# A two-layer graph, LSTM and max-plus network on one core: constants loaded one stage ahead, registers read first, dense rounds of two tokens

## The reference

```
x = x + gnn0(ln(x), adj)     # elu of gate * normed adj @ (x theta) + (1 - gate) * x W_h
x = x + lstm(ln(x))          # H = 256, then an argmax-gated prefix and suffix sum, * fw_att, bw_att
x = x + gnn1(ln(x), adj)     # D^-1/2 (adj + I) D^-1/2 (x W) + b
x = x + ffn(ln(x))           # below, FFN = 1024, 8 pieces
t[f]  = max_d(x[d] + Wt[f, d]) + bt[f]
trop  = s * max_p(t sl_cvx + of_cvx) + (1 - s) * min_p(t sl_ccv + of_ccv)
out   = (g * trop + (1 - g) * gelu(x Wc + bc)) @ Wd + bd,   g = sigmoid(x Wg + bg)
```

## Time and profile before

| | |
|---|---|
| median of 3 runs | 6029.61 us (6028.96 to 6030.96) |
| the profiled execution | 6013.3 us, its span 6011.5 us |
| busy: PE, DVE, ACT, POOL | 91%, 83%, 56%, 28% of the span |
| granted TensorE clock, mean | 0.965 |
| DMA moved | 529 MB, 88 GB/s over the span |
| stages, from the trace | first graph 0 to 525.6; recurrent to 1552.8; second graph to 2161.5; tropical to 4455.8 (slots from 3661.6 and 4163.4, dense from 4421.3); last to 6011.5 |

### The profile page before, as it was taken

The page is one execution under the profiler, slowest core; times in us unless marked ns, Lnnn a source line. Parts: engine busy times, 40 slices in busy tenths (PEclk is TensorE's granted clock), DMA queues, the critical chain, the costliest instruction groups (busy, mean ns, idle before and its releaser), DMA issues. The chain is left out here.

```text
span 6011.5 us, 111926 instructions
## 1 busy us (share of the span) xinstructions
PE 5471.9 (91%) x33194; PEld 3624.3 (60%) x33194; DVE 4967.6 (83%) x9615; ACT 3371.2 (56%) x6793; POOL 1711.0 (28%) x3552
## 2 busy tenths in 40 slices
PE   9998999999899969999999985875759999999999
PEld 6666888888788856666666653443434444444444
DVE  8996664444699969999999997986859999999998
ACT  6664444444455546666666651221228787877787
POOL 3331000000255536666666651375530000000000
PEclk9999999999899989999999997987979999999999
DMA  4442001000355522222222211365541212222221
GB/s 136 135 135 69 0 11 50 0 0 0 96 176 176 177 90 73 73 73 73 73 73 72 71 67 32 114 219 179 171 161 66 89 63 85 69 84 83 71 84 49
DMA packets 359806, 529.10 MB, mean 88 GB/s; under 512 B 28256, under 2 KB 298208, under 8 KB 359680
## 3 DMA queue, kind: packets, MB, share of 16 engines
q1 hardware_dynamic: 323376, 401.62, 20.5%
q0 software_dynamic: 36304, 126.13, 6.1%
HBM read 298.52 MB, written 229.14 MB: 88 GB/s over the span
## 5 line engine op out<-in xcount | busy, mean ns | idle before, releaser
L1894 PE MATMUL t_fetched<-t_wpart,t_onehot 128*128 128x512 f32 x4096 | 1222.0, 420 | 35.8 <-DVE t_tout L1999 15.9
L1999 DVE SCALAR_TENSOR_TENSOR t_tout<-t_fetched,t_top,t_tout 128x1024 f32<-128x1024 f32 x896 | 1149.0, 1282 | 36.3 <-PE t_fetched L1894 4.8
L1894 PEld LDWEIGHTS t_fetched<-t_wpart,t_onehot 128*128 128x128 f32 x4096 | 691.8, 188 | 269.2 <-DVE t_tout L1999 131.2
L2832 DVE SCALAR_TENSOR_TENSOR f_line<-f_hinge,f_vec,f_line 128x1024 f32<-128x1024 f32 x512 | 655.2, 1280 | 82.5 <-ACT f_hinge L2710 48.3
L2322 PE MATMUL ts_fetched<-t_wpart,ts_onehot 128*128 128x512 f32 x1608 | 508.7, 451 | 165.2 <-ACT ts_onehot L2297 65.3
L961 PE MATMUL l_ps<-l_wih,l_x 128*64 128x128 f32 (+1 forms) x6144 | 531.6, 308 | 1.0 <-DVE l_ps L597 1.0
L2322 PEld LDWEIGHTS ts_fetched<-t_wpart,ts_onehot 128*128 128x128 f32 x1608 | 305.6, 208 | 316.6 <-DVE ts_tout L2390 202.3
L961 PE MATMUL l_ps<-l_whh,l_ht 128*64 128x128 f32 (+1 forms) x6144 | 492.6, 309 | 0.0
L2762 PE MATMUL f_pso<-f_fused,f_wd 128*128 128x512 f32 x1024 | 461.9, 594 | 23.1 <-DVE f_ox L2828 23.1
L2749 PE MATMUL f_psc<-f_x,f_wc 128*128 128x512 f32 x1024 | 482.8, 594 | 0.0
L925 ACT ACTIVATE l_act<-l_ps 128x128 f32<-128x128 f32 x1024 | 253.9, 276 | 407.0 <-PE l_ps L961 407.0
(11 more groups left out here) (384 smaller groups left out, 10720.8 us busy)
## 6 DMA issues: line engine op xcount, KB each, us to landing
t<-t_tout SPq DMA_DIRECT2D x128, 512.0 KB, 2.6
f_t<-t SPq DMA_DIRECT2D x64, 1024.0 KB, 5.3
g_adj<-in_adj SPq DMA_DIRECT2D x128, 256.0 KB, 3.0
g_adjt<-in_adjt SPq DMA_DIRECT2D x128, 256.0 KB, 2.7
t_x<-x_normalised SPq DMA_DIRECT2D x130, 128.0 KB, 2.3
g_x<-in_x SPq DMA_DIRECT2D x64, 256.0 KB, 2.8
x_kept<-g_x SPq DMA_DIRECT2D x64, 256.0 KB, 2.1
g_x<-x_kept SPq DMA_DIRECT2D x64, 256.0 KB, 2.8
```

What stands on the lines that cost most here:

```text
L1894: mm = pe.matmul(fetched[c % RING][:, h * CH:(h + 1) * CH], one_hot[g][:, c % GRP * P:(c % GRP + 1) * P], w_part[part][:, k, h * CH:(h + 1 ...
L1999: dve.scalar_tensor_tensor(t_out[j][:, :], column[:, :], value, t_out[j][:, :], ALU.add, ALU.max)\
L2832: dve.scalar_tensor_tensor(acc[:, :], source, column(u, "bend", k), acc[:, :], ALU.mult, ALU.add)\
```

## The change

Four edits. The buffers of a stage's weights are allocated outside it, and their loads are issued by SP during the stage before: the recurrent weights and biases at the end of the first graph stage (its identity is kept for all three), the second graph stage's logit weights and `fw`, `bw` at the end of SP's program in the recurrent stage, and the last stage's six loads at the start of the dense block. In the second graph stage the first input now goes ahead of the five constants that are still loaded there, and PE and DVE wait for these inside their rounds, ahead of the first reader. The slot stages read the class ends (PE: candidate offsets too) before the first selection, and each engine only what it uses: ACT, DVE and POOL 11 instead of 16. In the last stage ACT and DVE read the counts ahead of the wait for the loads. A dense round takes 2 tokens instead of 8.

```diff
@@ -214,6 +213,14 @@
             for n in range(1, X_RING):
                 load(x_in, a["x"], x_loaded, n, n)
+            for w, name in ((w_ih, "w_ih_t"), (w_hh, "w_hh_t")):
+                sp.dma_start(w[:, :, :, :, :].rearrange("p k q c u -> p k (q c u)"),
+                             a[name].rearrange("(k p) g -> p k g", p=P)).then_inc(lstm_in, 16)
+            for e, name in enumerate(("b_ih", "b_hh")):
+                for c2 in range(2):
+                    half_rows = slice(c2 * (P // 2), (c2 + 1) * (P // 2))
+                    sp.dma_start(bias[half_rows, e, :, :].rearrange("p q u -> p (q u)"),
+                                 a[name][c2:c2 + 1, :].to_broadcast([P // 2, GATES * P])).then_inc(lstm_in, 16)
             for j in range(2):
...
@@ -533,15 +535,6 @@
         def _(sp):
-            for w, name in ((w_ih, "w_ih_t"), (w_hh, "w_hh_t")):
-                sp.dma_start(w[:, :, :, :, :].rearrange("p k q c u -> p k (q c u)"),
-                             a[name].rearrange("(k p) g -> p k g", p=P)).then_inc(const_in, 16)
-            sp.dma_start(ident[:, :], a["ident"]).then_inc(const_in, 16)
-            for e, name in enumerate(("b_ih", "b_hh")):
-                for c2 in range(2):
-                    sp.dma_start(bias[c2 * HB:(c2 + 1) * HB, e, :, :].rearrange("p q u -> p (q u)"),
-                                 a[name][c2:c2 + 1, :].to_broadcast([HB, GATES * P])).then_inc(bias_in, 16)
...
+            sp.dma_start(graph_consts["w_lin"][:, :, :], a["w_lin_t"].rearrange("(k p) c -> p k c", p=P))\
+              .then_inc(graph_consts["loaded"], 16)
+            for t in range(NT):
+                sp.dma_start(graph_consts["b_lin"][:, t, :], a["b_lin"].to_broadcast([P, 2])).then_inc(graph_consts["loaded"], 16)
+            for name, src in (("fw", a["fw_att"].to_broadcast([P, D])), ("bw", a["bw_att"].to_broadcast([P, D]))):
+                sp.dma_start(graph_consts[name][:, :], src).then_inc(graph_consts["loaded"], 16)
...
@@ -587,7 +586,7 @@
-            dve.wait_ge(bias_in, 16 * 4)
+            dve.wait_ge(lstm_in, 16 * 6)
             dve.tensor_tensor(bias_sum[:, :, :], bias[:, 0, :, :], bias[:, 1, :, :], ALU.add).then_inc(bias_ready, 1)
...
@@ -1007,7 +1006,7 @@
-            pe.wait_ge(const_in, 16 * 3)
+            pe.wait_ge(lstm_in, 16 * 6)
...
@@ -1111,7 +1106,7 @@
-        CONST_DMAS = 11
+        CONST_DMAS = 5
...
@@ -1135,17 +1130,6 @@
         def _(sp):
-            sp.dma_start(w_lin[:, :, :], a["w_lin_t"].rearrange("(k p) c -> p k c", p=P)).then_inc(const_in, 16)
-            sp.dma_start(ident[:, :], a["ident"]).then_inc(const_in, 16)
-            for t in range(NT):
-                sp.dma_start(b_lin[:, t, :], a["b_lin"].to_broadcast([P, 2])).then_inc(const_in, 16)
-                sp.dma_start(b_all[:, t, :], a["b1"].to_broadcast([P, D])).then_inc(const_in, 16)
-            sp.dma_start(fw[:, :], a["fw_att"].to_broadcast([P, D])).then_inc(const_in, 16)
-            sp.dma_start(bw[:, :], a["bw_att"].to_broadcast([P, D])).then_inc(const_in, 16)
-            sp.dma_start(before[:, :], a["before"]).then_inc(const_in, 16)
-            sp.dma_start(after[:, :], a["after"]).then_inc(const_in, 16)
-            sp.dma_start(w[:, :, :], a["W1"].rearrange("(k p) e -> p k e", p=P)).then_inc(const_in, 16)
             def load(dst, src, loaded, n, j):
...
-            for j in range(2):
-                load(x1_in, x1_dram, x1_loaded, j, j)
-                load(adj_in, a["adj"], adj_loaded, j, j)
-                load(adjt_in, a["adjt"], adjt_loaded, j, j)
+            load(x1_in, x1_dram, x1_loaded, 0, 0)
+            sp.dma_start(before[:, :], a["before"]).then_inc(late_in, 16)
+            sp.dma_start(after[:, :], a["after"]).then_inc(late_in, 16)
+            load(x1_in, x1_dram, x1_loaded, 1, 1)
+            for t in range(NT):
+                sp.dma_start(b_all[:, t, :], a["b1"].to_broadcast([P, D])).then_inc(late_in, 16)
+            load(adj_in, a["adj"], adj_loaded, 0, 0)
+            load(adjt_in, a["adjt"], adjt_loaded, 0, 0)
+            sp.dma_start(w[:, :, :], a["W1"].rearrange("(k p) e -> p k e", p=P)).then_inc(late_in, 16)
+            load(adj_in, a["adj"], adj_loaded, 1, 1)
+            load(adjt_in, a["adjt"], adjt_loaded, 1, 1)
             rounds(sp, body)
...
@@ -1295,6 +1286,7 @@
+                    pe.wait_ge(late_in, 16 * 5)
                     pe.wait_ge(wh_ready, n + 1)
...
@@ -1393,6 +1385,7 @@
+                    dve.wait_ge(late_in, 16 * 5)
                     dve.tensor_tensor(x2b[j][:, :, :], x2[:, :, :], b_all[:, :, :], ALU.add).then_inc(x2b_ready, 1)
...
@@ -1460,7 +1453,7 @@
-DENSE_RUN = 8
+DENSE_RUN = 2
...
@@ -2227,13 +2220,24 @@
-        def classes(eng, slot_pair):
-            ends = [eng.value_load(bounds[0:1, k:k + 1], min_val=2, max_val=MOST) for k in range(K)]
-            cands = [0] + [eng.value_load(bounds[0:1, K + k:K + k + 1], min_val=1, max_val=CLASSES[0] * MOST)
-                           for k in range(K - 1)]
-            hots = [0] + [eng.value_load(bounds[0:1, 2 * K - 1 + k:2 * K + k], min_val=1, max_val=CLASSES[0] * MOST)
+        def class_ends(eng):
+            return [eng.value_load(bounds[0:1, k:k + 1], min_val=2, max_val=MOST) for k in range(K)]
+        def class_cands(eng):
+            return [0] + [eng.value_load(bounds[0:1, K + k:K + k + 1], min_val=1, max_val=CLASSES[0] * MOST)
                           for k in range(K - 1)]
+        def class_hots(eng):
+            return [0] + [eng.value_load(bounds[0:1, 2 * K - 1 + k:2 * K + k], min_val=1, max_val=CLASSES[0] * MOST)
+                          for k in range(K - 1)]
+        unused = [0] * K
+        def classes(eng, ends, cands, hots, slot_pair):
...
+            ends = class_ends(pool)
             held(3, selected, 1)
             y_gather(0, rows[:, 2, 0:1])
-            end = classes(pool, slot_pair)
+            end = classes(pool, ends, class_cands(pool), unused, slot_pair)
...
-            classes(act, slot_pair)
+            classes(act, class_ends(act), unused, class_hots(act), slot_pair)
...
+            ends, cands = class_ends(pe), class_cands(pe)
             spread(0, 0, 0, 0, GRP)
-            classes(pe, slot_pair)
+            classes(pe, ends, cands, class_hots(pe), slot_pair)
...
+            ends = class_ends(dve)
             select(0, 0, 16, 2)
-            classes(dve, slot_pair)
...
+        @block.sync
+        def _(sp):
+            for w, at in ((early["w_raw"][0], AT_WC), (early["w_raw"][1], AT_WG), (early["w_d"], AT_WD)):
+                sp.dma_start(w[:, :, :], rows_dram[:, at:at + D].rearrange("(u p) d -> p u d", p=P)).then_inc(early["loaded"], 16)
+            sp.dma_start(early["ident"][:, :], a["ident"]).then_inc(early["loaded"], 16)
+            sp.dma_start(early["vec"][:, :, :], rows_dram[:, AT_VEC:ROW].rearrange("(u p) q -> p u q", p=P))\
+              .then_inc(early["loaded"], 16)
+            sp.dma_start(early["b_d"][:, :], a["bd"]).then_inc(early["loaded"], 16)
         @block.gpsimd
...
@@ -2620,14 +2629,6 @@
         def _(sp):
-            for v, at in ((0, AT_WC), (1, AT_WG)):
-                sp.dma_start(turned_in(v)[:, 0:FT, :],
-                             rows_dram[:, at:at + D].rearrange("(u p) d -> p u d", p=P)).then_inc(const_in, 16)
-            sp.dma_start(w_d[:, :, :], rows_dram[:, AT_WD:AT_WD + D].rearrange("(u p) d -> p u d", p=P)).then_inc(const_in, 16)
-            sp.dma_start(ident[:, :], a["ident"]).then_inc(const_in, 16)
-            sp.dma_start(vec[:, :, :], rows_dram[:, AT_VEC:ROW].rearrange("(u p) q -> p u q", p=P)).then_inc(const_in, 16)
-            sp.dma_start(b_d[:, :], a["bd"]).then_inc(const_in, 16)
...
@@ -2671,12 +2672,12 @@
         def _(act):
+            more, _ = counts(act)
             act.wait_ge(const_in, 16 * CONSTS)
             act.activation(half_bg[:, :], vec[:, :, 1], ACT.Copy, scale=0.5).then_inc(half_ready, 1)
             act.wait_ge(half_ready, 1)
             evict(act, 0)
-            more, _ = counts(act)
...
@@ -2796,9 +2797,9 @@
         def _(dve):
+            more, before = counts(dve)
             dve.wait_ge(const_in, 16 * CONSTS)
             evict(dve, 1)
-            more, before = counts(dve)
```

More of the change, by code:

```diff
@@ L79, in end, with stage_gnn0 @@
         assert self.k == self.per, (self.k, self.per)
-def stage_gnn0(nc, a, hx, x1_dram):
+def stage_gnn0(nc, a, hx, x1_dram, ident, w_ih, w_hh, bias, lstm_in):
     sems = []
@@ L449, with stage_lstm @@
 FAR = 1.0e30
-def stage_lstm(nc, a, hx, rows_dram, key_dram, hinge_count, row_kept):
+def stage_lstm(nc, a, hx, ident, w_ih, w_hh, bias, lstm_in, graph_consts, rows_dram, key_dram, hinge_count, row_kept):
     T, U = N, 4
@@ L457, in stage_lstm @@
     LANE = 384
-    sems = []
+    sems = [lstm_in]
     with ExitStack() as ctx:
@@ L465, in sem @@
             return sems[-1]
-        w_ih = sb("l_wih", [P, KD, GATES, 2, P])
-        w_hh = sb("l_whh", [P, KD, GATES, 2, P])
-        bias = sb("l_bias", [P, 2, GATES, P])
```

(38 more changed lines are left out.)

34 lines of the change are left out of this document (12 added, 22 removed).

## The result

| | before | after |
|---|---|---|
| median, five runs each | 6030.2 us (6028.96 to 6031.02) | **5996.95 us** (5994.34 to 6003.9) |
| profiled execution, span | 6013.3 us, 6011.5 us | 5996.85 us, 5995.0 us |
| mean granted TensorE clock | 0.965 | 0.965 |

The ratio is **0.9948, 95% interval 0.9933 to 0.9962**: faster, by about 33 us of the 50.9 forecast. On the scale of the first median, 6029.61, the ratio gives 5998.3, just above the range's end of 5998.

A forecast was written before the change was run, and what follows sets the result against it. Seams between stages, where TensorE idles for loads and register reads, were taken as the bound. Gains 5.6 + 8.9 + 12.1 + 13.0 + 11.3 = 50.9 us gave a profile of 5962.4, median 5979 us, range 5968 to 5998.

The forecast's parts named there:

- 1, first seam: First graph to recurrent stage: weights and biases issued behind the last store let PE start earlier; gain 5.6 us.
- 2, second seam: Recurrent to second graph stage: PE starts 9.9 us earlier, then stops 1.0 us for the late weight; gain 8.9 us.
- the waits in gnn1's loop: Second graph stage, two new waits in each of 64 rounds: taken as 0, at worst 4.5 us.
- 3, slots: Both slot stages: class bounds read ahead of the first selection bring first fetches forward 6.3 and 5.8 us; together 12.1.
- 4, dense uses: Dense block: two tokens a round leave 4 uses instead of 16, saving 12 steps, 14.6 us.
- 4, fill less gathers late: Dense block: shorter fill gains 0.4 us; gathers beside the last stage's loads come 2.0 us late.
- 5, last stage: Last stage's start: loads already landed and counts read first bring ACT's first line forward; gain 11.3 us, ends 9 and 13.
- a loop changing its pace: Sign against the forecast: it is wrong as a whole if a later stage's loop changes its pace.
- unfavourable end: Second seam's low case: the late weight lands when it did before, leaving a gain of 7.2 us.
- The slower rival: Second graph stage: fulfilled waits flush the engine, over 1.0 us a round makes the change slower; 6049 us at 1.1; 3%.
- The covers are short: Rival, 12%: DMAs moved into a stage delay it, losing 5.6, 3.0 and 1.7 us; gain 40.6 us, 5989 us.
- carried-over 16.3 us: Whole kernel: the median stood 16.3 us above the profiled execution, unexplained, and was assumed to do so again.

The follow-up runs named there:

- e6: Changed kernel plus idle instructions, 6 on DVE in the tropical constants and 30 on ACT in the dense block; 5968.91 us, ratio 0.992.
- e4: Kernel before plus only the slot stages' earlier register reads and the dense round of two tokens; 5993.98 us, ratio 0.9963.
- e10: Changed kernel plus `w` loaded behind the first x1, idle instructions (6 DVE, 30 ACT), last stage's loads issued in the tropical plan's block; 5961.03 us, ratio 0.9909.
- e3: Kernel before plus only the earlier loads for the recurrent and second graph stages; 6009.54 us, ratio 0.999.
- e12: Kernel before plus idle instructions, 4 on DVE ahead of `tropical_first` and 64 on ACT in the dense block; 6019.65 us (a single run).
- e5: Kernel before plus idle instructions, 10 on DVE in the tropical constants and 98 on ACT in the dense block; 6026.85 us, ratio 1.0016.

## Why the prediction was right and wrong

The terms, each as the mean over the profiles without and with the edit (14 in all):

| step | forecast | measured | from |
|---|---|---|---|
| 1, first seam | 5.6 | 5.0 | last copy to first gate 23.5 to 18.6 |
| 2, second seam | 8.9 | 6.7 | last hidden state to first `g_xn3t` 50.0 to 43.3 |
| the waits in gnn1's loop | 0 | -1.1 | loop 554.9 to 556.05 |
| third seam | 0 | -0.4 | last `g_xn3t` to first merge 47.2 to 47.6 |
| 3, slots | 12.1 | 11.9 | 96.1 to 89.8, and 34.2 to 28.6 |
| 4, dense uses | 14.6 | 14.3 | first to last use 20.3 to 6.0 |
| 4, fill less gathers late | 0.4 - 2.0 | -2.4 | last slot to first use 26.2 to 28.6 |
| 5, last stage | 11.3 | 10.6 | last use to ACT's first line 32.0 to 21.3 |
| loops not touched | 0 | -5.7 and -6.0 | `tropical_first` 1381.0 to 1386.6; ffn 1405.45 to 1411.5 |
| **sum** | **50.9** | **32.9** | the medians: 33.3 and 32.4 |

**The step that failed** is the sentence under the first bold words: the change leaves the bodies of the long loops as they are, so the forecast is a sum over five places. The bodies stayed, their places in the streams did not, and that cost 11.7 of the 18.0 us missing. The prediction named a loop changing its pace as what would make it wrong as a whole, but gave the untouched loops no term and no rival. The other 6.3 us are in the terms themselves: 2.2 in step 2, 1.1 in the loop's waits, 0.8 in the gathers and the fill, the rest in pieces under 1 us. Put right by idle instructions alone, the change gives 48.6 us (e6), but 3 of these come from an ffn loop that is even shorter than that of before. The five places by themselves measured 46.1 us, a tenth less than the 50.9 forecast.

**Step 1** was right in its mechanism: SP's stream does not hold the block for the landing. PE's last release is the bias, as said. It came out 0.6 short. The openers start 6.9 us behind ACT's last copy on average over the nine profiles with the edit, where the forecast has 6.5, and 12.1 in the five without. "No better after 6 us" was right for the level (granted 0.50), but its length differs between executions: where it lasts 13.7 us (four profiles) the seam takes 17.4 to 17.9 us, where it lasts 17.1 (five) 19.0 to 19.7. Without the edit it lasts 20.5 in all five. The 8.41 us of the openers in the row above belong to the second kind; the mean is 7.77 us with the edit and 7.65 without, so the clock explains the scatter here and little of the mean shortfall.

**Step 2** mis-sized one term: the stop for `w`, 1.0 forecast, was 2.4 to 3.8 us in the five profiles with `w` late. The prediction took 5.2 us from issue to landing from the row of before, where `w` was last behind small constants; here x1, adj and its transpose are ahead of it and it took 6.8 to 8.2. A landing time taken from one row holds only for the queue ahead of it in that row. Putting `w` first removed the stop for `w` and left one of 0.8 to 2.2 us for the bias rows, which gave about 1 us. The "unfavourable end" of 7.2 did not hold this either (6.7).

**The loop's waits**: 0 taken, 4.5 the end, about 1 measured: 0.017 us a round, waits and place together. The slower rival's flush of 1.0 us a round is out.

**Steps 3 and 5** held within 0.7 us; 0.65 us for each bounded register read was the right price.

**Step 4**: with 12 uses fewer the last fetch comes when the clock is low, and DVE waits 1.17 us for it instead of 0.30, as warned (granted 0.50 from 4432 to 4437). The gathers: with the short fill and no loads beside them the stretch is 25.7 us (e4, e10), with the loads 28.6, so they were late by 2.9. That lies between the 1.7 at which only their own bytes come on top and the 5.0 at which they land with the loads, nearer to the first; the step took 2.0. The changed kernel's DMA issues from 4420 to 4436 (count, KB, us from issue to landing) show what they did not wait for:

```profile
f_wraw<-per_f_sorted SPq DMA_DIRECT2D x2, 1024.0 KB, 7.6
f_wd<-per_f_sorted SPq DMA_DIRECT2D x1, 1024.0 KB, 12.0
```

`f_wd`, issued at 4421.81, ahead of the gather at 4424.15, landed at 4433.8; DVE had its rows at 4431.3. The taking of turns between queues that the Trainium skill states ("DMA: Bandwidth & Descriptors", queues, rings and completion order) fits this, with more loss than the 1.7 that the prediction estimated by it. The Trainium skill's sentence on semaphores (same section), as the prediction read it, would have put DVE behind 4433.8, and the trace does not show that.

**The rivals.** "The covers are short" forecast 5989 and stood nearest to the result, mostly by luck. The largest of its three parts, 5.6 us at the end of the first stage, did not happen; of the 3.0 for the gathers 0.9 did; only the third did in full, the late weight, with 2.2 us instead of 1.7. The rest of the way to the result are the untouched loops, which it did not have. The carried-over 16.3 us between profile and median did not hold as a gap: the changed kernel's first profile stands 0.1 us from its median, and its slot halves hold 18 us that no other profile has. The difference of the two medians is free of it, as both are of the same chip. Nothing in the kernels explains it: on other chips the same kernel's median is 6016 to 6018.

## What to carry to other kernels

When an edit adds or removes instructions ahead of a long loop, look at that loop's length in both traces before explaining the total. A stop ended by "issue" once per pass with packets of the instruction queue beside it, or a few hundredths of a microsecond per round, may be a cost of where the code lies. Idle instructions placed under a wait test that, and can give it back. Judge such an edit by its seam and the loops apart, since a lucky or unlucky place can hide or fake several microseconds. A load that is put into another queue position needs its landing worked out anew from what is ahead of it.

## What the runs showed of the hardware that was not expected

- The place of a loop in an engine's stream costs 5.7 us in 1381 (DVE, 0.4%) and 6 to 9 us in 1405 (ACT, 0.4 to 0.7%), repeatably and with nothing between; 98 and 10 idle instructions alone made the kernel before 0.16% slower.
- The ffn loop of before was not at its best either: every second block took 95.0 us, the others and those of e6 94.6 (first `f_ox` to first `f_ox`). That 0.38 goes away with other places too (e3, e6, e12). Which engine's it is was not tried.
- In the first profile of after, five 3.4 us stretches of half clock lay in the ffn loop, 191 us apart, each behind a stop of ACT. e5 has the same stops, no such stretch, and the same loop time (1412.0): the stops cost the time, not the clock.
- Fulfilled waits are nearly but not quite free: about 1 us for two in each of 64 rounds, the effect on the place of the code behind them included.
